# Four pieces for each of the two wide one-hot comparisons of a step, with a release per group

## What is computed

```python
edge_index = jnp.stack([src, dst])
x = _layernorm(x + L0(x, edge_index, edge_attr_16, ...))   # segment_sum((x@W)[src] * (edge_attr@edge_w), dst) + b
x = _layernorm(x + L1(x, edge_index, ...))                 # (segment_sum(x[src], dst) / deg) @ W_l.T + b_l + x @ W_r.T
x = _layernorm(x + L2(x, edge_index, ...))                 # segment_sum(x[src] * edge_norm, dst) @ weight + bias
x = _layernorm(x + L3(x, edge_index, ...))                 # normalised sum, tanh, gate, relu, batch norm
```

## Time and profile before

| | |
|---|---|
| time, median of 2 runs | 3636.62 us (3635.95 to 3637.29) |
| time of the profiled execution | 3642.16 us |
| its span | 3639.8 us |
| mean granted TensorE clock | 0.783 |
| busy share PE, DVE, ACT, POOL | 71%, 43%, 15%, 56% |

### The profile page before, as it was taken

One profiled execution on the slowest core, in us unless ns is written; L12 is line 12 of the kernel. 1 busy time (PEld: TensorE's weight loads), 2 busy tenths in 40 slices (PEclk: granted clock), 3 DMA queues, 4 the chain that ended last, 5 costly groups with the idle time before them and its releaser, 6 DMA issues.

```text
span 3639.8 us, 35592 instructions
## 1 busy us (share of the span) xinstructions
PE 2578.6 (71%) x12818; PEld 1594.3 (44%) x12818; DVE 1574.8 (43%) x2392; ACT 530.3 (15%) x1141; POOL 2024.1 (56%) x1703
## 2 busy tenths in 40 slices
PE   3566666766666666666667676765799899879980
PEld 2344444444444444444444444443444444545540
DVE  3455555455545454545454545454311311231136
ACT  0111111111111111111111111110200300111112
POOL 6777777777777777777777777773100200000001
PEclk7777777777777777777777777776899999889995
DMA  5222222222222222222222222226177577627641
GB/s 177 72 83 81 86 82 86 81 87 86 78 85 86 82 85 83 85 86 81 83 83 82 86 82 85 84 83 178 73 289 295 223 295 294 239 106 282 270 163 35
DMA packets 215777, 462.28 MB, mean 127 GB/s; under 512 B 43877, under 2 KB 84042, under 8 KB 215386
## 3 DMA queue, kind: packets, MB, share of 16 engines
q1 hardware_dynamic: 159358, 344.17, 25.4%
q0 software_dynamic: 54480, 112.65, 12.3%
q10 hardware_dynamic: 1804, 3.72, 0.3%
HBM read 372.09 MB, written 88.32 MB: 126 GB/s over the span
## 4 chain that ended last, share of the span: by engine, by line
POOL 51%; PE 25%; issue 16%; DVE 5%; another core or an unknown queue 1%; DMA 1%; ACT 1%; DVEq 0%; ACTq 0%; POOLq 0%; SPq 0%
POOL big L563 49%; PE pb L1032 11%; PE pb L1033 11%; PE pb L1007 1%; PE pb L1041 1%; POOL big L543 1%; POOL y L547 1%; DMA big<-at 0%; DVE y L886 0%; ACT tmp L1133 0%; PE pb L970 0%; DVE tmp L770 0%; DVE big L652 0%; PE pb L1057 0%
## 5 line engine op out<-in xcount | busy, mean ns | idle before, releaser
L563 POOL DMA_INDIRECT big<-xw,big x1612 | 1910.4, 1185 | 501.0 <-issue 490.9
L970 PE MATMUL pb<-big 128*128 128x64 f32 x3232 | 635.1, 378 | 638.8 <-DVE big L677 618.3
L970 PEld LDWEIGHTS pb<-big 128*128 128x128 f32 x3232 | 599.8, 286 | 671.6 <-DVE big L677 649.9
L677 DVE TENSOR_TENSOR big<-pb,big 128x512 f32<-128x512 f32 x404 | 261.3, 687 | 1103.5 <-DMA big<-xw,big 1059.0
L1032 PE MATMUL pb<-big,yT 128*128 128x512 f16 (+1 forms) x1911 | 688.0, 368 | 23.1 <-DMA big<-at 17.5
L930 PE MATMUL pb<-big 128*128 128x512 f32 x808 | 672.7, 982 | 24.4 <-DVE ident L615 24.4
L1033 PE MATMUL pb<-big,yT 128*128 128x512 f16 (+1 forms) x1911 | 687.8, 368 | 0.0
L1099 ACT CAST tmp<-pb 128x392 f16<-128x392 f32 x784 | 349.8, 488 | 1740.9 <-PE pb L947 1056.1
L652 DVE TENSOR_TENSOR big<-cols_p,big 128x2048 f16<-128x2048 f16 x196 | 447.9, 2285 | 0.8
L947 PE MATMUL pb<-big 128*128 128x98 f16 x3136 | 247.2, 212 | 173.7 <-ACT tmp L1099 80.8
L654 DVE TENSOR_TENSOR big<-cols_key,big 128x1568 f16<-128x1568 f16 x196 | 349.6, 1784 | 0.0
(11 more groups left out here) (145 smaller groups left out, 1008.0 us busy)
## 6 DMA issues: line engine op xcount, KB each, us to landing
big<-at SPq DMA_DIRECT2D x36, 6272.0 KB, 18.0
at<-tmp SPq DMA_DIRECT2D x196, 392.0 KB
big<-xw,big POOLq DMA_INDIRECT x1612
big<-in_ea SPq DMA_DIRECT2D x202, 64.0 KB
big<-at SPq DMA_DIRECT2D x3, 1568.0 KB, 6.6
xw<-big SPq DMA_DIRECT2D x7, 448.0 KB
x<-tmp POOLq DMA_DIRECT2D x7, 448.0 KB, 7.3
out<-tmp SPq DMA_DIRECT2D x6, 448.0 KB, 3.0
```

The costliest lines, as they stand in the source:

```text
L563: nc.gpsimd.indirect_dma_start(gath[:, T8 * (n % NG) + t % T8, :], None, xw_d, bass.IndirectOffsetOnAxis(ap=src_i[:, t:t + 1], axis=0)).th ...
L677: nc.vector.tensor_tensor(msg[:, T8 * (n % 2) + 4 * q:T8 * (n % 2) + 4 * q + 4, :], PB[:, q, :].rearrange("p (t f) -> p t f", f=D), gath[: ...
L970: last = nc.tensor.matmul(PB[:, 2 + n % 2, 0:WIN], msg[:, T8 * (n % 2) + t, :], hot_win[:, T8 * (n % 2) + t, :], start=(t == 0), stop=(t = ...
```

## The change

`hots(j)` goes through the four groups of four pairs. For each group it compares 4 x 128 elements of `hot_lo` and then 4 x 98 of `hot_key`, and releases `s_hot`. So there are eight instructions for two, and four releases for one. Ahead of each group it waits for PE's products of the same group of tile j-2, where it waited for all of tile j-2. PE waits ahead of each group for that group's release, where it waited once for the tile's. No operand, type or place in memory changes.

```diff
             def hots(j):
                 b, c = j // BL, j % BL * NPR
-                if j >= 2:
-                    v.wait_ge(s_amm, GA * (j - 1))
                 v.wait_ge(s_lk, b + 1)
                 at_pair = NPR * (j % 2)
-                nc.vector.tensor_tensor(hot_lo[:, at_pair:at_pair + NPR, :], cols_p[:, :].unsqueeze(1).broadcast_to([P, NPR, P]),
-                                        lokeyT[:, b, c:c + NPR].unsqueeze(2).broadcast_to([P, NPR, P]), ALU.is_equal)
-                nc.vector.tensor_tensor(hot_key[:, at_pair:at_pair + NPR, :], cols_key[:, :].unsqueeze(1).broadcast_to([P, NPR, KW]),
-                                        lokeyT[:, b, P + c:P + c + NPR].unsqueeze(2).broadcast_to([P, NPR, KW]), ALU.is_equal).then_inc(s_hot, 1)
+                for g in range(GA):
+                    if j >= 2:
+                        v.wait_ge(s_amm, GA * (j - 2) + g + 1)
+                    here, there = slice(at_pair + GP * g, at_pair + GP * g + GP), slice(c + GP * g, c + GP * g + GP)
+                    keys = slice(P + c + GP * g, P + c + GP * g + GP)
+                    nc.vector.tensor_tensor(hot_lo[:, here, :], cols_p[:, :].unsqueeze(1).broadcast_to([P, GP, P]),
+                                            lokeyT[:, b, there].unsqueeze(2).broadcast_to([P, GP, P]), ALU.is_equal)
+                    nc.vector.tensor_tensor(hot_key[:, here, :], cols_key[:, :].unsqueeze(1).broadcast_to([P, GP, KW]),
+                                            lokeyT[:, b, keys].unsqueeze(2).broadcast_to([P, GP, KW]), ALU.is_equal).then_inc(s_hot, 1)
...
             def a_products(j):
-                pe.wait_ge(s_hot, j + 1)
                 for g in range(GA * j, GA * j + GA):
+                    pe.wait_ge(s_hot, g + 1)
                     if g >= 2:
                         pe.wait_ge(s_aev, g - 1)
```

## The result

The changed kernel took 3735.74 us (3729.14 to 3742.35, 2 runs) against 3636.62: 1.027 of the kernel before, 95% interval 1.019 to 1.035. I had forecast 3430 us, faster by 5.7%, with a range of 3385 to 3520. It came out slower, by 2.7%.

What follows compares the result with a forecast made beforehand. POOL's gathers were taken to bound the first stage; cutting their stretch from 1.96 to 0.90 us over 196 steps saves 208 us, giving 3430 us (-5.7%) from the median of 3636.6, range 3385 to 3520.

Steps and rivals of the forecast that it cites:

- What stretches a gather: POOL's gathers in the first stage: a VectorE comparison holds one until that instruction ends; 384 us of stretch, 1.96 per step.
- The inferred exception for `tensor_tensor`: Skill's inference that `tensor_tensor` leaves DMA issue alone, so the split gains nothing, 3637; the prediction held the trace against it.
- The pieces' length: VectorE's comparison pieces: 0.68 and 0.556 us each, 0.38 us more per step, covered by its wait for gathered rows.
- What a gather now waits: POOL's gathers held by the shorter pieces: between 0.70 and 1.18 us per step, taken as 0.90, where it was 1.96.
- The waits that are added: Three more waits each on VectorE and PE per tile, for things long done: zero cost.
- what comes next when POOL is faster: First-stage step falls from about 12.0 to 10.9 us; PE's mean chain 9.2, VectorE 6.3, so POOL stays the bound.
- PE takes over: Rival: the step cannot shrink below PE's chain; a step of 11.4 us would give 3519 us; 7 in 100.
- The rival on the slow side: Pieces take the port ahead of the waiting gather at each boundary: 1.7 us more per step, 3970 us; 4 in 100.
- The range: 3385 to 3520 us, from bounds of 0.70 us and three caught asks per step, with the PE case at its edge.

Runs made afterwards that it cites:

- the pieces with one release: Changed kernel's eight comparison pieces, but one release and one PE wait per tile, as in the kernel before: 0.939 on chip K, 1.019 on chip M.
- the short lead: Changed kernel with POOL allowed three steps ahead of VectorE's messages instead of four: 0.941 on chip K, 1.028 on chip M.
- The four waits on PE alone: Kernel before, wide comparisons kept, with PE's wait for `s_hot` moved inside the loop over groups: 1.001 on chip K.
- small writes behind the gathers: Eight pieces, one release per tile, plus a 0.45 us POOL write behind every gather from step 4: 1.070 on chip O, 1.065 on chip N.
- The pause of 1.1 us: Changed kernel plus two small POOL writes behind the fourth gather of each step from step 4: 0.9705 on chip K, 1.020 on chip N.

## Why the prediction was wrong

*What stretches a gather: right.* The held gather goes at the end of the piece that holds it, with 0.82 us left, in both kinds of chip (in the changed kernel the piece that starts at 1141.69 ends at 1142.37, and the gather that it held at 1143.19). The Trainium skill, page "SBUF — State Buffer", section "Who interferes with whom", has VectorE's instruction with two SBUF inputs block a GpSimd instruction that reads SBUF until it ends, and the trace agrees, 0.81 and 0.82 us in the rows above. The inferred exception for `tensor_tensor` in the same section has fallen: cutting it up took 224 us from the gathers.

*The pieces' length: right.* 682 and 558 ns, forecast 0.68 and 0.556.

*What a gather now waits: right in size.* 155 us of stretch over 196 steps is 0.79 us per step where I had taken 0.90. On a chip without late releases the whole sum holds: 0.939 for the pieces with one release and 0.941 for the short lead, forecast 0.943.

*The waits that are added: right, nearly.* The four waits on PE alone cost 0.1%. Four releases or one took 0.941 and 0.939 on chip K (the first with the shorter lead too), and 1.026 and 1.019 on chip M.

*The step that failed is "what comes next when POOL is faster".* I set PE's chain at 9.2 us per step, from its mean wait of 2.9 us, and let it stay there. That took PE's work and the trips between PE, ScalarE and VectorE as a fixed length. A step has several such trips: the edge products to the messages, the window product to `window_add`, the products to the eviction and back to the next group. In the recorded comparison and on chips L, M, N and P, each trip could find its release late, and more often so the denser POOL's gathers were. The chain is then longer than POOL's step: VectorE no longer waits for gathered rows (13.3 us where it was 902.4) but for PE's releases (685.0 us in `window_add` where it was 17.4). The rival "PE takes over" had the right engine and the wrong reason and size: it held the chain's length fixed, and so could not go beyond no gain.

The sign was in the trace before: a release 35.6 us late at 126.23, in the first steps, where no wide comparison holds the gathers. And ScalarE's 92.8 us for "remote" in 41 places, and PE standing for up to 9.7 us behind the evictions, are rows that I passed over because they lay off the chain. How often they come depends on POOL's stream, which the change alters.

*The rival on the slow side* named the gather as shut out by the pieces. It was not: the longest gather fell from 2.96 to 1.46 us.

*The range* was wrong in kind. It was built from bounds on POOL's stretch, with the case of a fixed chain on PE at its edge, and had no case in which what POOL does changes what another engine needs.

Shown: that the same kernel takes 0.939 on one chip and 1.019 on another, with late releases only on the second; that the waits and the releases added are not the main cause; that VectorE's number of instructions is at most a small part; that small writes behind the gathers remove the late releases after the first steps on a chip that has them. Argued only: that it is the density of the stream, and that the long hold in the kernel before works by the break it makes. The pause of 1.1 us didn't help, and no pause as long as the hold was tried. Open: by what path gather issues keep PE's releases back, why a thinned stream does not free one that is held, and why some chips were free of it. Chip N had late releases on two occasions; K and O were each seen on one, so whether a chip keeps its kind isn't known. The ends of products in a profile are modelled, and by them alone a release that was held can't be told from one that was given late.

## What to carry to other kernels

When an engine's issue stream is made denser, look at what else its gaps let through: a wait whose releaser the profile can't name, however small, is to be read before the change and not after. A chain through several engines has the length of its releases as well as of its work, so a mean wait is no proof of room. Look also at stretches where the stream already runs as densely as the change will make it; here the first four steps of the kernel before were one. And a gain or loss of a few per cent on such a chain should be timed on more than one chip, since here the same kernel was 6% faster on one and 2% slower on another.

## What the runs showed of the hardware that I had not expected

PE's semaphore releases reached ScalarE, VectorE and the DMA queue more than 30 us after the product had ended (32 us at 1139.75 in the changed kernel, 35.6 us at 126.23 in the kernel before), often several of them at one moment, on chips L, M, N and P and in the recorded comparison; on chips K and O no wait for "remote" appeared anywhere in the traces of the seven kernels that ran there. VectorE's longest waits ended after POOL had run out of work, and with one step less of lead they were 11.1 us shorter. The Trainium skill, page "SBUF — State Buffer", section "Who interferes with whom", also says that PE and ACT never wait on anyone. Its concern is the SBUF port, and no run here shows PE waiting for that; but PE stood 28 us in one place here, behind ScalarE, to which its own releases had not come through while POOL issued gathers.

A comparison of one element with both inputs in SBUF did POOL no harm that shows: six of them per step left the gathers at 1900.8 us on chip O, against 1905.4 without on chip K, both without late releases.
